# A three-layer graph network on one Trainium2 core: 16 dense chunks moved from the second and third mean pass into the first, with a new layout of PSUM banks and small tables

## The chip, the cores and the metric

The program runs on one core of a Trainium2 chip. The time is the device time of one execution in microseconds (us); a lower time is better. The engines are PE (TensorE, matmuls), DVE (VectorE), ACT (ScalarE), POOL (GpSimd, here mainly the issuer of indirect transfers) and SP (SyncE, the issuer of plain transfers). Each works through its own instruction queue in order and waits there on semaphores.

## What is computed

There are 50,000 nodes with 128 features and 25,000 edges (`src`, `dst`). Two parts follow one another, each with a residual and a row-wise layer norm:

```python
def _sage_conv(x, src, dst, Wl, bl, Wr):
    msg = x[src]
    summed = jax.ops.segment_sum(msg, dst, num_segments=N_NODES)
    cnt = jax.ops.segment_sum(jnp.ones((src.shape[0],), x.dtype), dst, num_segments=N_NODES)
    mean = summed / jnp.maximum(cnt, 1.0)[:, None]
    return mean @ Wl.T + bl + x @ Wr.T
...
x = _layernorm(x + three _sage_conv with relu between them)
x = _layernorm(x + edge attention, summed by src and projected)
```

The second part gathers queries, keys and values per edge, takes a softmax over the edges of each source node and adds the result to the node. The change lies in the first part alone.

## The kernel before

Work is cut into chunks of 512 rows (4 tiles of 128). 25,000 edges make 49 edge chunks (`NC`), 50,000 nodes make 98 node chunks (`NN`). The program has these stages: a sort of the edges by destination and by source; three **mean passes** `mean0`, `mean1`, `mean2`, one per layer; a pass `dst` over the nodes that receive edges; `attend`; and `rest`. The change touches the three mean passes and shares its helpers with `dst`.

**A mean chunk.** POOL gathers 4 tiles of source rows into `GX` (`mean_gather`, L675; `GX` has 8 slots, so POOL can be 8 chunks ahead). PE turns them (`mean_turn`: transposes at L774 in `mean0`, a matmul L890 and L892 in the later passes). DVE makes a running sum within each destination (`mean_seg`, L1396). ACT copies the turned rows into `hsrc` (`mean_keep`). PE multiplies by the left weights (`mean_prod`, L900), DVE divides by the edge count (`mean_scale`, L1403), SP stores the result. In `mean0` ACT's copy comes after the scan, in the later passes before it.

**A look-up chunk**, in `mean0` and `dst`. DVE makes one-hot rows (`look_hot_rows`, L1440), PE multiplies them with a small table (`look_up`, L929), DVE picks four columns (`look_take`, L1449) and casts them into `lookup` (L1456), which the gathers of `mean1` and `mean2` use. Before the first look-up of `mean0` a table is made on DVE and PE (`make_table`, `table_sums`); it is passed to `run` as `middle`.

**A dense chunk** treats 512 nodes that receive no edge: load of `x` (SP), transposes (`chain_t`, L774), two layers (`chain_1`, `chain_2`, L852), the last layer (`chain_y`, L870 and L872), each with an ACT copy between them; then DVE adds `x` (`add_x`, L1350), measures (L1358, L1363), ACT takes the inverse root, DVE normalises (`norm`, L1374), and SP stores. The first 49 dense chunks run in `mean1`, the other 49 in `mean2`, none in `mean0`.

**What sets the order.** `run(eng, phase, stages, count)` writes one software pipeline per engine: in step s it emits, for each stage (lead, function), the function for chunk s + lead, in the order of the list. On PE in `mean0` a step is turn(s+7), look-up(s), product(s+6); on DVE scan(s+7), scale(s+6), one-hot(s+1), take(s). In `mean1` and `mean2` the dense stages lead by 6 to 9 steps and the turn by 3, so that after the last dense `chain_y` only the turns of the last 3 chunks are left. A wait is written as a signal and how many chunks ago it must have been given: `look_up` in `mean0` waits for the take of 2 chunks ago, since it writes banks (0, 1) and (6, 7) in turn:

```python
pe.wait_ge(look_hot.of(c), look_hot.after(c))
pe.wait_ge(look_done.of(c), look_done.after(c, 2 if c.phase == "mean0" else 1))
```

The small tables and one-hot rows lie in the space of `XN`, the buffer of the dense chunks' rows, which is why SP loads no `x` before the last take of `mean0` (`look_done.end(sp, "mean0")`). Between two passes POOL waits until every product is stored (`m_stored.end`).

## Time and profile before

| | us |
|---|---|
| median of 3 runs | 2648.06 (2647.51 to 2650.15) |
| the profiled execution, its own time | 2644.61 |
| its span | 2642.8 |
| PE busy | 1873.9 (71%) |
| DVE busy | 1729.4 (65%) |
| ACT busy | 1095.2 (41%) |
| POOL busy | 1770.9 (67%) |

These are means over stages with different limits. The running sums of `mean0` start between 192.1 and 420.0 us of the span; the gathers of `mean1` begin at 429.3, those of `mean2` at 760.1, those of `dst` at 1069.5, and the last stage ends at the span's end. The granted clock of PE was 0.854 of full speed over the span. Of a row below, the first number is the start in us, the second how long the engine was busy with the group; what stands in brackets is the idle time just before it and what ended it.

### The profile page before, as it was taken

To read this page: it belongs to the slowest core of one execution; us is meant where nothing else is said; L and a number is where in the kernel's file an instruction comes from. 1 tells how busy PE (TensorE), PEld (TensorE's weight loads), DVE (VectorE), ACT (ScalarE), POOL (GpSimd) and SP (SyncE) were. 2 spreads that over 40 slices of the span, in tenths; PEclk is the share of its full clock that TensorE was granted. 3 is DMA by queue.
4 is the path that set the end of the run, shared out by engine and by line. 5 is a ranking of instruction groups with operands and counts; after the bars stand their busy time and mean duration, and the time that the engine had idled before them with its cause. 6 is when DMAs were issued, how large, how long until landed. Compare 5 with 4: busy or idle time off the path is not lost.

```text
span 2642.8 us, 43434 instructions
## 1 busy us (share of the span) xinstructions
PE 1873.9 (71%) x10441; PEld 1316.8 (50%) x10441; DVE 1729.4 (65%) x5671; ACT 1095.2 (41%) x2508; POOL 1770.9 (67%) x1895
## 2 busy tenths in 40 slices
PE   4755666999989999677777673888788877770000
PEld 2324565666656666455555453555555555540000
DVE  7787886777767777565555533888888878881000
ACT  7951111544534444122222222777666666650000
POOL 0046776566756676467777777777777777766776
PEclk7558999999999999788888885999999999995555
DMA  0025666788877887545445623455445445433321
GB/s 19 1 56 148 165 159 138 174 195 189 177 172 187 189 192 173 154 125 135 126 128 142 164 68 106 144 158 157 144 143 152 145 140 152 140 104 104 94 92 51
DMA packets 366730, 357.03 MB, mean 135 GB/s; under 512 B 46534, under 2 KB 288724, under 8 KB 366584
## 3 DMA queue, kind: packets, MB, share of 16 engines
q1 hardware_dynamic: 310136, 246.40, 31.0%
q0 software_dynamic: 56448, 109.10, 20.3%
q14 instruction: 106, 0.87, 0.1%
q8 instruction: 40, 0.66, 0.1%
HBM read 232.83 MB, written 129.11 MB: 137 GB/s over the span
## 4 chain that ended last, share of the span: by engine, by line
PE 32%; POOL 26%; issue 17%; DVE 13%; DMA 5%; ACT 5%; POOLq 1%; DVEq 0%; SPq 0%; ACTq 0%
POOL GX L675 10%; POOL hsrc L675 9%; PE bank L852 9%; PE bank L872 5%; POOL out_dram L729 4%; PE bank L774 3%; PE bank L900 3%; PE bank L892 3%; PE bank L890 3%; DMA GX<-in_x_dram,idx_a 3%; PE bank L856 2%; ACT normed L1021 2%; ACT normed L1022 2%; DVE stats L1358 2%; POOL x_prime L729 2%
## 5 line engine op out<-in xcount | busy, mean ns | idle before, releaser
L675 POOL DMA_INDIRECT GX<-mean_product,idx_a x392 | 411.2, 1049 | 129.5 <-issue 113.9
L675 POOL DMA_INDIRECT GX<-in_x_dram,idx_a x392 | 378.1, 965 | 117.9 <-issue 108.9
L852 PE MATMUL bank<-h,wt 128*128 128x512 f32 x588 | 321.0, 657 | 0.1
L1046 ACT ACTIVATE logv<-mv,eps 128x4 f32<-128x4 f32 x245 | 72.2, 295 | 541.5 <-DVE mv L1363 541.4
L729 POOL DMA_INDIRECT x_prime<-normed,idx_b x196 | 197.6, 1008 | 88.0 <-issue 83.4
L729 POOL DMA_INDIRECT out_dram<-XN,idx_b x196 | 192.8, 984 | 76.0 <-issue 64.8
L675 POOL DMA_INDIRECT hsrc<-x_prime,idx_d x196 | 189.7, 968 | 59.7 <-issue 59.7
L675 POOL DMA_INDIRECT GX<-in_edge_attr_dram,idx_a x196 | 189.7, 968 | 58.6 <-issue 53.5
L675 POOL DMA_INDIRECT hsrc<-x_prime,idx_c x196 | 186.7, 953 | 59.7 <-issue 59.7
L774 PE MATMUL bank<-ident,GX 128*128 128x128 f32 x588 | 104.5, 307 | 155.5 <-DMA GX<-in_x_dram,idx_a 149.5
L774 PE MATMUL bank<-ident,hsrc 128*128 128x128 f32 x468 | 86.5, 316 | 119.0 <-DMA hsrc<-x_prime,idx_d 57.4
L872 PE MATMUL bank<-wt,h 128*128 128x128 f32 x1176 | 170.3, 288 | 0.0
L1139 ACT ACTIVATE normed<-bank,shift,rstd 128x128 f32<-128x128 f32 x392 | 147.7, 457 | 44.9 <-DVE shift L1553 44.9
L900 PE MATMUL bank<-wt,seg 128*128 128x128 f32 x1176 | 158.5, 278 | 7.0 <-DVE seg L1396 3.6
L1374 DVE TENSOR_SCALAR normed<-res,mv,rstd 128x128 f32<-128x128 f32 x588 | 163.1, 344 | 0.0
L1345 DVE TENSOR_TENSOR res<-bank,GX 128x512 f32<-128x512 f32 x49 | 33.9, 691 | 196.9 <-PE bank L872 196.6
L856 PEld LDWEIGHTS bank<-ident,hsrc 128*128 128x128 f32 x784 | 129.0, 233 | 67.4 <-issue 67.4
L774 PEld LDWEIGHTS bank<-ident,GX 128*128 128x128 f32 x588 | 73.9, 155 | 171.6 <-issue 88.3
L774 PE MATMUL bank<-ident,XN 128*128 128x128 f32 x784 | 130.2, 293 | 41.0 <-DMA XN<-x_prime 24.2
L872 PEld LDWEIGHTS bank<-wt,h 128*128 128x128 f32 x1176 | 142.3, 191 | 33.3 <-issue 33.3
L1396 DVE TENSOR_TENSOR_SCAN seg<-flag,seg,hsrc 128x512 f32<-128x512 bf16 x98 | 126.1, 1286 | 48.0 <-ACT hsrc L1061 48.0
L900 PEld LDWEIGHTS bank<-wt,seg 128*128 128x128 f32 x1176 | 144.2, 193 | 9.0 <-DVE seg L1396 8.6
(231 smaller groups left out, 4656.0 us busy)
## 6 DMA issues: line engine op xcount, KB each, us to landing
mean_product<-prod SPq DMA_DIRECT2D x147, 256.0 KB, 4.3
hsrc<-mean_product SPq DMA_DIRECT2D x147, 256.0 KB, 4.4
XN<-in_x_dram SPq DMA_DIRECT2D x98, 256.0 KB, 4.5
x_prime<-normed SPq DMA_DIRECT2D x98, 256.0 KB
XN<-x_prime SPq DMA_DIRECT2D x98, 256.0 KB, 4.5
out_dram<-normed SPq DMA_DIRECT2D x98, 256.0 KB
flag<-same_dst_row SPq DMA_DIRECT2D x147, 128.0 KB, 4.3
XN<-low_row SPq DMA_DIRECT2D x98, 128.0 KB
```

What stands on the lines that cost most here:

```text
L675: pool.indirect_dma_start(buf[:, c.slot(U), t, :], None, table, bass.IndirectOffsetOnAxis(ap=idx[:, c.slot(U), t:t + 1], axis=0)).then_inc ...
L729: pool.indirect_dma_start(table, bass.IndirectOffsetOnAxis(ap=idx_b[:, c.slot(U), t:t + 1], axis=0), rows[:, t, :], None, bounds_check=N - ...
L774: return pe.transpose(dst, src, ident[0:src.shape[0], 0:src.shape[0]])
L852: last = pe.matmul(psum[:, :], wt[:, T_R[i], :], before[:, c.slot(2), :], start=True, stop=not dst_phase)
L856: last = pe.matmul(psum[:, t * P:(t + 1) * P], PL[:, c.slot(U), i, t, :], ident[:, :], start=False, stop=t == TPC - 1)
L872: last = pe.matmul(y[:, t * P:(t + 1) * P], h2[:, c.slot(2), t * P:(t + 1) * P], wt[:, T_R[2], :], start=False, stop=t == TPC - 1)
L890: pe.matmul(psum[:, :], wt[:, T_R[i], :], take_cols(hsrc, c.index() * CH, CH), start=True, stop=False)
L892: last = pe.matmul(psum[:, t * P:(t + 1) * P], GX[:, c.slot(U), t, 0:D], ident[:, :], start=False, stop=t == TPC - 1)
L900: last = pe.matmul(bank[3 + c.slot(2)][:, t * P:(t + 1) * P], seg[:, c.slot(2), t * P:(t + 1) * P], wt[:, T_L[int(c.phase[-1])], :], start ...
L1139: last = act.activation(normed[:, node.slot(4), t, :], norm_rows(node)[:, t, :], ACT.Identity, bias=shift[:, s, t:t + 1], scale=rstd[:, s, ...
L1374: last = dve.tensor_scalar(normed[:, c.slot(4), t, :], norm_rows(c)[:, t, :], mv[:, s, t, 0:1], rstd[:, s, t:t + 1], ALU.subtract, ALU.mult)
L1396: dve.tensor_tensor_scan(seg[:, c.slot(2), :], flag[:, c.slot(4), :], rows, seg[:, before.slot(2), CH - 1:CH], ALU.mult, ALU.add).then_inc ...
```

## The change

1. `BEFORE = 16` dense chunks run in `mean0`, (98 - 16) / 2 = 41 in each of `mean1` and `mean2` (49 before).
2. In `mean0` all mean and look-up stages lead by 5 more steps (`TABLE = 5`), so the dense chunks 0 to 15 come behind the table; `middle` is placed by a new argument `at`.
3. PSUM: the dense chunks need banks 0, 1, 2 and 6 in `mean0`. So the turn has bank 5 alone (5 and 2 before), the product bank 3 alone in `mean0` (3 and 4), the look-up banks 4 and 7 alone (two pairs before), the dense result bank 6 alone in `mean0`.
4. The waits follow: the turn waits for the copy and the scan of 1 chunk ago, the look-up for the take of 1 chunk ago (2 before), the product for the scale of 1 chunk ago in `mean0`.
5. The one-hot rows move into `res` and have one buffer instead of two, in `mean0` and in `dst`; the tables move out of `XN` into the spent raw weights. SP's wait for the last take ahead of the loads of `mean1` goes away.

```diff
@@ run
-def run(eng, phase, stages, count, to_end=True, middle=None):
+def run(eng, phase, stages, count, to_end=True, middle=None, at=0):
...
     for s in range(-max(lead for lead, _, _ in stages), 0):
+        if middle and s == -at:
+            middle()
         single(s)
-    if middle:
-        middle()
...
+    EACH = (NN - BEFORE) // 2
...
+        low_all = sb("low_all", [P, 2, CH], BF16)
+        picked = sb("picked", [P, TPC, WIDE], BF16)
+        spent = wraw[:, 0:6, :].rearrange("p a d -> p (a d)")
...
+        hot = res[:, 2, :, :].rearrange("p t d -> p (t d)").bitcast(BF16).rearrange("p (a n) -> p a n", a=2)
...
-        def turn_bank(c):
-            return (5, 2)[c.slot(2)]
+        def prod_bank(c):
+            return bank[3] if c.phase == "mean0" else bank[3 + c.slot(2)]
+        def y_bank(c):
+            return bank[6] if c.narrow else bank[6 + c.slot(2)]
...
         def first(f):
-            return lambda c: f(At("dense", c.j, c.u))
+            return lambda c: f(At("dense", c.j, c.u + BEFORE))
...
-            run(sp, "mean0", [(LAG + 3, flag_load), (2, low_load), (LAG, prod_store)], NC)
-            look_done.end(sp, "mean0")
+            run(sp, "mean0", [(TABLE + LAG + 3, flag_load), (TABLE + 2, low_load), (TABLE + LAG, prod_store),
+                              (8, zeroth(x_load), BEFORE), (0, zeroth(x_store), BEFORE)], NC)
...
             def mean_turn(c):
                 pe.wait_ge(gathered.of(c), gathered.after(c))
+                pe.wait_ge(m_h.of(c), m_h.after(c, 1))
                 if c.phase == "mean0":
-                    pe.wait_ge(m_h.of(c), m_h.after(c, 2))
-                    pe.wait_ge(m_seg.of(c), m_seg.after(c, 2))
+                    pe.wait_ge(m_seg.of(c), m_seg.after(c, 1))
+                psum = bank[5]
...
             def mean_prod(c):
                 pe.wait_ge(m_seg.of(c), m_seg.after(c))
-                pe.wait_ge(m_scaled.of(c), m_scaled.free(c))
+                pe.wait_ge(m_scaled.of(c), m_scaled.after(c, 1 if c.phase == "mean0" else 2))
...
             def look_banks(c):
-                return ((0, 1), (6, 7))[c.slot(2)] if c.phase == "mean0" else (3, 4)
+                return (4, 7) if c.phase == "mean0" else (3, 4)
             def look_up(c):
                 pe.wait_ge(look_hot.of(c), look_hot.after(c))
-                pe.wait_ge(look_done.of(c), look_done.after(c, 2 if c.phase == "mean0" else 1))
+                pe.wait_ge(look_done.of(c), look_done.after(c, 1))
...
-                    run(pe, "mean0", [(LAG + 1, mean_turn), (0, look_up), (LAG, mean_prod)], NC, middle=table_sums)
+                    run(pe, "mean0", [(TABLE + LAG + 1, mean_turn), (TABLE, look_up), (TABLE + LAG, mean_prod),
+                                       (4, zeroth(chain_t), BEFORE), (3, zeroth(chain_1), BEFORE),
+                                       (2, zeroth(chain_2), BEFORE), (1, zeroth(chain_y), BEFORE)], NC,
+                        middle=table_sums, at=TABLE + 1)
...
-                    run(act, "mean0", [(0, mean_keep)], NC)
+                    run(act, "mean0", [(TABLE + LAG + 1, mean_keep), (4, zeroth(keep_t), BEFORE), (3, zeroth(keep_1), BEFORE),
+                                        (2, zeroth(keep_2), BEFORE), (1, zeroth(inverse_root), BEFORE)], NC)
...
             def look_hot_rows(c):
                 s = c.slot(2)
                 dve.wait_ge(low_in.of(c), low_in.after(c))
-                dve.wait_ge(look_sum.of(c), look_sum.after(c, 2))
+                dve.wait_ge(look_sum.of(c), look_sum.after(c, 1))
...
-                    run(dve, "mean0", [(LAG + 1, mean_seg), (LAG, mean_scale), (1, look_hot_rows), (0, look_take)], NC,
-                        middle=make_table)
+                    run(dve, "mean0", [(TABLE + LAG + 1, mean_seg), (TABLE + LAG, mean_scale), (TABLE + 1, look_hot_rows),
+                                        (TABLE, look_take), (1, zeroth(add_x), BEFORE), (0, zeroth(norm), BEFORE)], NC,
+                        middle=make_table, at=TABLE + 1)
```

The stage lists of `mean1` and `mean2` differ only in the count `EACH` behind each dense stage.

How the order changes on PE inside `mean0`. Before, two steps of the loop (L774 turn, L929 look-up, L900 product):

```order
L774 MATMUL bank2<-ident,GX 128x128 x4
L929 MATMUL bank0<-XN 128x196 x8
L929 MATMUL bank1<-XN 128x196 x8
L897 REGISTER_ALU
L900 MATMUL bank3<-wt,seg 128x128 x4
L774 MATMUL bank5<-ident,GX 128x128 x4
L929 MATMUL bank6<-XN 128x196 x8
L929 MATMUL bank7<-XN 128x196 x8
L897 REGISTER_ALU
L900 MATMUL bank4<-wt,seg 128x128 x4
```

Of the change, one step that carries a dense chunk, and the start of the next (L777 is the transpose, L855 the two layers, L873 and L875 the last layer of the dense chunk):

```order
L777 MATMUL bank5<-ident,GX 128x128 x4
L929 MATMUL bank4<-wraw,res 128x196 x8
L929 MATMUL bank7<-wraw,res 128x196 x8
L900 MATMUL bank3<-wt,seg 128x128 x4
L777 MATMUL bank0<-ident,XN 128x128 x4
L855 MATMUL bank1<-h0,wt 128x512
L855 MATMUL bank2<-h1,wt 128x512
L873 MATMUL bank6<-b2row,ones3 128x512
L875 MATMUL bank6<-wt,h2 128x128 x4
L777 MATMUL bank5<-ident,GX 128x128 x4
L929 MATMUL bank4<-wraw,res 128x196 x8
L929 MATMUL bank7<-wraw,res 128x196 x8
```

The look-up stands ahead of the product in both. Its banks were (0, 1) and (6, 7) in turn and are 4 and 7 in every step now, and the dense matmuls stand behind the product in 16 of the steps.

On DVE, of the change, a step of `mean0` with a dense chunk (L1402 scan, L1409 scale, L1446 one-hot, L1455 take, L1462 cast, L1356 add, L1364 and L1369 measure, L1380 normalise):

```order
L1402 SCALAR_TENSOR_TENSOR seg<-flag,seg,bank5 128x512
L1409 TENSOR_TENSOR prod<-bank3,col_f 128x512
L1446 TENSOR_SCALAR res<-low_all,low_bias 128x512 x2
L1455 SCALAR_TENSOR_TENSOR picked,wraw<-count,wraw,bank4 128x196 x2
L1455 SCALAR_TENSOR_TENSOR picked,wraw<-count,wraw,bank7 128x196 x2
L1462 CAST lookup<-wraw 128x4
L1356 TENSOR_TENSOR res<-bank6,XN 128x512
L1364 BN_STATS stats<-res 128x6 x4
L1369 BN_AGGR mv<-stats 128x2 x4
L1380 TENSOR_SCALAR normed<-res,mv,rstd 128x128 x4
```

The first six rows stand in every step as before; the last four are new there and stand behind the cast.

## Rows read from the trace of the kernel before

**Rows 1.** Windows of `mean0` and `mean1`: length, busy us per engine, PE clock, DMA share, GB/s

```profile
core 0: us, PE busy (x) PEld busy (x) DVE busy (x) ACT busy (x) POOL busy (x), PEclk, DMA share, GB/s
223.00:420.00 197.00, 129.87 (x1168) 118.86 (x1169) 163.76 (x534) 24.49 (x41) 145.82 (x162) 0.95 0.63 158
466.00:753.00 287.00, 285.60 (x1621) 197.52 (x1620) 226.14 (x697) 135.84 (x272) 181.14 (x179) 1.00 0.82 183
```

**Rows 2.** Timeline of `mean0`, one step: scale, one-hot, look-up, cast, next scale

```profile
352.45 0.67 DVE L1403 TENSOR_TENSOR prod<-bank,col_f 128x512 f32<-128x512 f32 x1
353.03 0.68 DVE L1440 TENSOR_SCALAR XN<-XN,low_bias 128x512 bf16<-128x512 bf16 x2
...
354.49 1.53 PE L929 MATMUL bank<-XN 128*128 128x196 bf16 x16
...
355.31 0.17 DVE L1456 CAST lookup<-XN 128x4 f32 x1 [0.24 <-DVE XN L1449]
...
357.11 0.69 DVE L1403 TENSOR_TENSOR prod<-bank,col_f 128x512 f32<-128x512 f32 x1 [0.25 <-PE bank L900]
```

**Rows 3.** Timeline of `mean1`, one full step on PE and DVE

```profile
600.02 1.88 PE L852 MATMUL bank<-h,wt 128*128 128x512 f32 x4
...
603.15 1.06 PE L900 MATMUL bank<-wt,seg 128*128 128x128 f32 x8
...
603.35 0.69 DVE L1350 TENSOR_TENSOR res<-bank,XN 128x512 f32<-128x512 f32 x1 [0.76 <-PE bank L872]
...
605.39 1.11 DVE L1374 TENSOR_SCALAR normed<-res,mv,rstd 128x128 f32<-128x128 f32 x4
...
605.79 0.60 PE L774 MATMUL bank<-ident,XN 128*128 128x128 f32 x4
...
606.23 1.88 PE L852 MATMUL bank<-h,wt 128*128 128x512 f32 x4
```

**Rows 4.** Timeline around the table in `mean0`

```profile
209.43 0.65 DVE L1440 TENSOR_SCALAR XN<-XN,low_bias 128x512 bf16<-128x512 bf16 x2 [2.58 <-DMA XN<-low_row]
...
222.91 0.06 DVE L1433 MEMSET XN<- 128x1 f32 x1
...
231.60 1.28 DVE L1396 TENSOR_TENSOR_SCAN seg<-flag,seg,bank 128x512 f32<-128x512 bf16 x1
```

**Rows 5.** Timeline from the last gather of `mean0` to the first transposes of `mean1`

```profile
411.33 0.94 POOL L675 DMA_INDIRECT GX<-in_x_dram,idx_a  x1 [0.30 <-issue]
...
419.95 1.28 DVE L1396 TENSOR_TENSOR_SCAN seg<-flag,seg,bank 128x512 f32<-128x512 bf16 x1
...
424.93 0.69 DVE L1403 TENSOR_TENSOR prod<-bank,col_f 128x512 f32<-128x512 f32 x1 [0.88 <-PE bank L900]
...
440.69 0.17 DVE L1456 CAST lookup<-XN 128x4 int32<-128x4 f32 x1 [0.15 <-DVE XN L1449]
...
443.95 1.09 PE L774 MATMUL bank<-ident,XN 128*128 128x128 f32 x4 [4.90 <-DMA XN<-in_x_dram]
```

**Rows 6.** Timeline of the end of `mean1`: scans 39, 46 and 48, gather of chunk 43

```profile
706.14 1.32 DVE L1396 TENSOR_TENSOR_SCAN seg<-flag,seg,hsrc 128x512 f32<-128x512 bf16 x1 [0.36 <-ACT hsrc L1061]
...
706.20 0.96 POOL L675 DMA_INDIRECT GX<-mean_product,idx_a  x1 [0.60 <-POOL idx_a L665]
...
746.80 1.28 DVE L1396 TENSOR_TENSOR_SCAN seg<-flag,seg,hsrc 128x512 f32<-128x512 bf16 x1 [0.18 <-ACT hsrc L1061]
...
752.51 1.28 DVE L1396 TENSOR_TENSOR_SCAN seg<-flag,seg,hsrc 128x512 f32<-128x512 bf16 x1 [0.99 <-ACT hsrc L1061]
```

**Rows 7.** Timeline of the head of `dst`: a cast and the look-up behind it

```profile
1100.36 0.17 DVE L1456 CAST lookup<-XN 128x4 int32<-128x4 f32 x1 [0.15 <-DVE XN L1449]
...
1100.67 1.87 PE L929 MATMUL bank<-dst_table,XN 128*128 128x256 bf16 x8 [2.20 <-DVE lookup L1456]
```

**Rows 8.** PE at either clock: a look-up right after the table, and two windows

```profile
224.31 2.82 PE L929 MATMUL bank<-XN 128*128 128x196 bf16 x16
...
250.00:260.00 10.00, 5.78 (x56) 5.31 (x56) 9.30 (x31) 1.79 (x3) 7.56 (x9) 1.00 0.74 179
1080.00:1100.00 20.00, 9.33 (x40) 5.17 (x40) 10.36 (x48) 0.00 (x0) 15.43 (x18) 0.50 0.35 94
```

More of the change, by code:

```diff
@@ L38 @@
 DENSE = 5
+BEFORE = 16
+TABLE = 5
 LINE = 256
@@ L138, in run @@
     for s in range(-max(lead for lead, _, _ in stages), 0):
+        if middle and s == -at:
+            middle()
         single(s)
-    if middle:
-        middle()
-    with eng.Fori(0, whole) as j:
-        for u in range(U):
-            for lead, f, _ in stages:
-                f(At(phase, j, u + lead))
+    if whole:
+        with eng.Fori(0, whole) as j:
+            for u in range(U):
+                for lead, f, _ in stages:
+                    f(At(phase, j, u + lead))
     for s in range(whole * U, count):
@@ L867, in chain_y @@
                 pe.wait_ge(u2_kept.of(c), u2_kept.after(c))
-                pe.wait_ge(added.of(c), added.free(c))
-                y = bank[6 + c.slot(2)]
+                pe.wait_ge(added.of(c), added.after(c, 1 if c.narrow else 2))
+                y = y_bank(c)
                 pe.matmul(y[:, :], ones3[:, :], b2row[:, :, :].rearrange("k t d -> k (t d)"), start=True, stop=False)
@@ L1340, in add @@
                 s = c.slot(2)
-                y = by_tile(bank[6 + c.slot(2)][:, :])
+                y = by_tile(y_bank(c)[:, :])
                 dve.wait_ge(y_done.of(c), y_done.after(c))
@@ L1387, in mean_seg @@
                     dve.wait_ge(m_turned.of(c), m_turned.after(c))
-                    rows = bank[turn_bank(c)][:, :]
+                    rows = bank[5][:, :]
                 else:
```

69 lines of the change are left out of this document (29 added, 40 removed).

## The prediction

> **What bounds the kernel now.** I read the windows of the stages first, since the page's busy shares are means over stages with different limits. In `mean1` PE is busy 285.60 of 287.00 us at full clock, and `mean2` is the same pass again [rows 1]. So a dense chunk taken out of `mean1` or `mean2` shortens PE's queue at the bound. In `mean0` PE is busy 129.87 of 197.00 us and DVE 163.76 [rows 1]: 67 us free on PE, 33 on DVE. That is the room into which the change puts 16 dense chunks. POOL's gathers cost 0.94 + 0.31 us each, 5.0 per chunk (rows 5 show the last one of `mean0`); POOL also sets the pace of the second half of `mean0`. Second view: the timeline of one step in each pass, for the loops of waits between PE and DVE. Third: the two ends of the passes, for who is late there.
>
> The sum is made in the profiled execution (2644.61 us, span 2642.8), and 3.4 us are added at the end for the median (2648.06).
>
> **A loop closes in `mean0`.** Before, the look-up on PE runs while DVE still takes the previous one, since it has a second pair of banks. In the change it waits for that take and its cast. PE's queue then has look-up and product, and DVE's next scale waits for the product; behind the scale stand one-hot, take and cast, and the cast releases the next look-up. Each link has a row. From scale to the cast's end: 352.45 to 355.48, 3.03 us. From look-up to the next scale, released by PE's product: 354.49 to 357.11, 2.62 us [rows 2]. From a cast to the look-up that waits for it: `dst` already has this wait, 1100.53 to 1100.67, 0.14 us [rows 7]. Sum 5.8 us per step. The scan (1.28 us) hides behind look-up and product.
>
> Rule against row: the Trainium skill ("TensorE: Matmul & The Clock Gate", section "HAM oscillation — how this bites in real kernels") reports a kernel in which double-buffering PSUM "gave no further gain"; by that, taking the second banks away would cost nothing, which is the third rival below. No run here shows it yet.
>
> **A step with a dense chunk** has on DVE, behind the cast, add to normalise: 603.35 to 606.50, 3.15 us [rows 3]. DVE's queue is then 1.28 + 3.03 + 3.15 = 7.46 us. PE's is turn 0.60, look-up 1.53, product 1.06 and dense 603.15 - 600.02 = 3.13 plus its transposes 0.60, together 6.9 us [rows 2, 3]. DVE is the longer, and PE's dense matmuls cover the wait of the loop. So 7.46. The first dense step has no normalise: 1.28 + 3.03 + 2.04 = 6.35. The last has only a normalise (1.11 us), which fits into the 5.8. The single turn bank costs nothing while the copy (behind the scan) ends some 3 us ahead of the next look-up; if it did not, PE would start the look-up late and every step would pay.
>
> **Sum for `mean0`, from scan 8 on.** Before, scan 8 starts at 231.60 [rows 4] and scan 48 at 419.95 [rows 5], 188.35 us for 40 steps.
> - Table. The step behind the table has one scan and scale fewer ahead of it and the one-hot behind it. DVE is free at 209.43 - 2.58 = 206.85 [rows 4]; less that scan, scale and their wait, 2.3, the table begins at 204.55 in place of 210.0, 5.4 earlier, but about 3.2 of scan, scale, one-hot and waits come behind it. Scan 8: 2.2 us earlier.
> - 40 steps: 24 x 5.8 + 6.35 + 15 x 7.46 = 257.4, in place of 188.35: +69.1.
> - Scan 48 to scale 48: before 4.98 (419.95 to 424.93); now one loop to the cast (5.8) and 0.14 + 2.62: 8.5, +3.5. POOL's gathers of `mean1` wait for this product.
> - The six last look-ups: before, the last cast ends at 440.86, 15.9 behind scale 48 [rows 5]. Now scale to cast 3.03 and six times look-up 1.53, two latencies of 0.1, one-hot, take and cast 2.45 (353.03 to 355.48), 4.2 us, less 0.6 as the last has no one-hot: 27.6, +11.7.
> - The rows `x` for `mean1` are loaded ahead now. Before, PE's first transposes start 3.1 us behind the last cast and end a wait for that DMA [rows 5]; now about 0.2: -2.9. SP has five stages per step in its queue: the store of a dense chunk waits for the normalise, and the low-row load of the next step stands behind it; it is needed a full step (over 5 us) later, so nothing.
>
> Together the first dense work of `mean1` starts 79.2 us later. POOL starts its gathers 70.4 later and has its 8 slots full before PE asks, so it is covered.
>
> **Sum for `mean1` and `mean2`.** A full step is 6.21 us (600.02 to 606.23) [rows 3]. Eight fewer put the last step with dense work at 746.80 - 49.7 = 697.1, in the times of before. From there 10 more turns at (752.51 - 746.80) / 2 = 2.86 us [rows 6] would end at 725.7. But POOL is late next: the gather of chunk 43 starts when turn 39 frees its slot (706.20 beside scan 39 at 706.14 [rows 6]), then 5 more at 5.02, and from the start of a last gather to its scan 8.6 us (411.33 to 419.95 [rows 5]), some 1.1 more here, as turn and copy come ahead of the scan. 697.1 + 2.9 + 25.1 + 9.7 = 734.8 in place of 752.51: 17.7 us per pass, 35.4 for both. Unhidden ends for this: 26.8 per pass (POOL not late), and 12 if the gathers keep the 6 us that many have under load. I take 17.7, since rows 5 are a drained tail like this one.
>
> **`dst`.** The one-hot has one buffer and now stands in the loop of look-up and cast: 0.34 us [rows 2] for the 7 look-ups ahead of the first dense work: +2.4.
>
> **Total:** 79.2 - 35.4 + 2.4 = +46.2 us. 2644.6 + 46.2 = 2690.8; with the 3.4 of the median 2694.
>
> **Bounds.** A mean-only step of `mean0` is between DVE's busy time, 163.76 / 41 = 4.0 us [rows 1], and 8.1, the loop at half clock (below). I take 5.8, the sum of its links. A dense step is between 6.9 (PE) and 8.5 (a wait of 1 us at each end of the add).
>
> **Rivals.**
> - *PE's clock falls (slower).* In the loop PE is busy 3.2 of 5.8 us. At 5.78 of 10 us it still had the full clock of 2.4 GHz, at 9.33 of 20 it had 0.50, 1.2 GHz [rows 8], and after an idle stretch a look-up took 2.82 us in place of 1.53. If it stays down, 24 steps cost 1.29 + 1.06 more each, +56 us: 2750; half of that if it swings. The last six look-ups are the likeliest place: 1.3 each, 8 us. The Trainium skill (same page, section "A second HAM failure mode: psum-queue depth-cycling") says short pauses between groups of matmuls make the clock swing; the row with 5.78 speaks against it here.
> - *POOL is not late at the ends of `mean1` and `mean2`.* 26.8 per pass in place of 17.7: 2676. Against it stands the free-running pitch of 5.0 us, beside 2.86.
> - *The loop stays open (faster).* If the second buffers were idle slack, DVE's queue alone would set `mean0`: 24 x 4.0 and 16 x 7.15 make 210.4, +22; nothing for the six look-ups. -2.2 + 22.0 - 2.9 - 35.4 + 2.4 = -16.1: 2632. With the measured 4.3 us of an unblocked step it would be 2643, no difference. The point of decision is a mean-only step of 4.3 us: above it the change is slower. For it speaks that the dense work does go to a stage with 67 us of free PE time; against it, that `dst` shows this very wait, 2.20 us idle ahead of each look-up [rows 7].
>
> **Chances.** Forecast 0.68 (its own range 2680 to 2712), clock 0.14, POOL not late 0.10, loop open 0.08. The range 2664 to 2730 takes in the second rival and half of the first; it leaves out the open loop, the full clock loss and a few errors of size. A measurement of this kernel can tell 0.2%, 5 us, from no change. Faster 0.06 and same 0.03 are the open loop at its two prices, with a little for an error in the sum; slower 0.91.
>
> **What the profile of the changed kernel would show.** Casts of `mean0` 5.8 us apart without and 7.5 with a dense chunk; PE idle before each look-up, released by the cast (DVE), not the one-hot; scale released by PE's product. The gathers of `mean1` start near 500 us, first transposes at 523. In `mean1` and `mean2` 32 full steps of 6.2, then turns at 2.9, then at 5 waiting for the gather DMA; first gathers of `mean2` near 820, of `dst` near 1113. `attend` unchanged. The prediction is wrong if scans of `mean0` come 4.3 us apart in mean-only steps, if they come 7 to 8 apart with the clock near 0.5, or if the last turns of `mean1` never wait for POOL.

## The result and the profile after

The changed kernel takes 2736.48 us (median of 6 runs, 2732.89 to 2739.44) where the kernel before, on the same chip, takes 2648.57 (6 runs, 2646.49 to 2652.07): ratio 1.033, 95% interval 1.0317 to 1.0343. It is slower, as forecast, but by 88 us where the forecast had 46, and outside its range. The profiled execution takes 2734.38 us with a span of 2732.1; the span of before is 2642.8, so 89.3 us are to be placed.

The page of the changed kernel first: busy times, the PE clock in 40 slices, and three groups of its fifth part (busy and mean ns of one, then the idle time before them and what ended it).

```profile
PE 1908.8 (70%) x10441; PEld 1345.7 (49%) x10441; DVE 1732.4 (63%) x5671; ACT 1092.1 (40%) x2508; POOL 1774.0 (65%) x1895
...
PEclk7568987799998999878888887799999999995555
...
L678 POOL DMA_INDIRECT GX<-mean_product,idx_a x392 | 409.2, 1044 | 126.6 <-issue 110.9
L678 POOL DMA_INDIRECT GX<-in_x_dram,idx_a x392 | 379.5, 968 | 122.8 <-issue 109.1
...
L929 PE MATMUL bank<-wraw,res 128*128 128x196 bf16 x784 | 106.4, 309 | 92.2 <-DVE lookup L1462 91.9
```

DVE is as busy as before (1732.4 against 1729.4): nothing was added to its work. PE has 35 us more (1908.8 against 1873.9) for the same matmuls, and sits idle for 92.2 us ahead of the look-ups of `mean0`. A busy time that grows without new work is a sign of a lower clock, and the windows show where. Columns as in [rows 1].

```profile
core 0: us, PE busy (x) PEld busy (x) DVE busy (x) ACT busy (x) POOL busy (x), PEclk, DMA share, GB/s
240.00:360.00 120.00, 106.87 (x756) 79.95 (x755) 109.90 (x416) 44.41 (x94) 65.28 (x72) 1.00 0.59 168
360.00:507.00 147.00, 89.12 (x590) 80.85 (x588) 89.64 (x299) 13.04 (x23) 69.24 (x77) 0.77 0.46 114
571.00:848.00 277.00, 263.13 (x1483) 184.31 (x1482) 202.63 (x593) 117.34 (x233) 181.41 (x179) 0.98 0.82 174
506.00:549.00 43.00, 21.33 (x144) 18.07 (x144) 19.95 (x94) 0.60 (x1) 20.75 (x24) 0.71 0.52 121
```

The first is `mean0` with dense chunks, the second `mean0` without, the third `mean1`, the last the six look-ups at the end of `mean0`. With dense chunks beside it PE keeps 1.00. Without, and among the last look-ups, it gets 0.77 and 0.71, between its two levels of 1.2 and 2.4 GHz (0.50 and 1.00), where before the whole of `mean0` had 0.95 [rows 1].

| span from, to | before | after | difference | forecast |
|---|---|---|---|---|
| start to scan 8 | 231.6 | 229.7 | -1.9 | -2.2 |
| 40 steps, scan 8 to scan 48 | 188.4 | 277.5 | +89.1 | +69.1 |
| scan 48 to the last cast | 20.7 | 42.2 | +21.5 | +15.2 |
| last cast to scan 0 of `mean1` | 25.0 | 22.0 | -3.0 | -2.9 |
| `mean1`, scan 0 to scan 48 | 286.8 | 277.2 | -9.7 | -17.7 |
| `mean2`, the same | 286.8 | 277.3 | -9.5 | -17.7 |
| between the passes, `dst` and the rest | | | +2.8 | +2.4 |
| sum | 2642.8 | 2732.1 | +89.3 | +46.2 |

The form of the forecast holds in every line. 26.5 of the 43 us that it lacks are in `mean0`, 16.2 at the ends of `mean1` and `mean2`.

**A step without a dense chunk.** Timeline of the changed kernel; [rows 2] show one of before.

```profile
458.86 0.37 DVE L1462 CAST lookup<-wraw 128x4 int32<-128x4 f32 x1
459.06 1.28 DVE L1402 TENSOR_TENSOR_SCAN seg<-flag,seg,bank 128x512 f32<-128x512 bf16 x1
...
459.38 2.77 PE L929 MATMUL bank<-wraw,res 128*128 128x196 bf16 x16 [2.85 <-DVE lookup L1462]
...
461.94 1.24 PE L900 MATMUL bank<-wt,seg 128*128 128x128 f32 x8
...
463.22 0.69 DVE L1409 TENSOR_TENSOR prod<-bank,col_f 128x512 f32<-128x512 f32 x1 [2.88 <-PE bank L900]
463.82 0.61 DVE L1446 TENSOR_SCALAR res<-low_all,low_bias 128x512 bf16<-128x512 bf16 x2
```

This is the loop of the forecast, link by link: PE waits 2.85 us for the cast, DVE waits 2.88 us for the product, one at a time. But the look-up takes 2.77 us where the forecast had 1.53, much as the first look-up behind the table did before (2.82 us, [rows 8]). Most such steps are 6.8 to 7.1 us apart, 6.78 on average.

This is not a clock that is down in one step and up in the next. Of the look-ups 21 to 41 of `mean0`, 16 of 21 take 2.77 us and one takes 1.52 (mean 2.64); the products behind them take 1.39 us on average where 1.06 to 1.08 is the time at full clock and 1.92 to 1.96 at half. So in nearly every step the look-up, right behind the wait, runs at half clock, and the product mostly at full clock again.

**The same loop stood in the trace of before.** At the head of `dst` each look-up waits for a cast, 2.20 us, and takes 1.87 us [rows 7]; the clock granted from 1100 to 1108 us is 0.50. A few steps on, with dense work on PE and no wait, the same eight matmuls need little more than half. Timeline of before:

```profile
1109.37 1.04 PE L929 MATMUL bank<-dst_table,XN 128*128 128x256 bf16 x8
```

So the kernel before already had the price of a look-up behind such a wait.

**A step with one.** Same view, 150 us earlier:

```profile
312.05 0.17 DVE L1462 CAST lookup<-wraw 128x4 int32<-128x4 f32 x1
312.15 0.69 DVE L1356 TENSOR_TENSOR res<-bank,XN 128x512 f32<-128x512 f32 x1
312.37 1.52 PE L929 MATMUL bank<-wraw,res 128*128 128x196 bf16 x16 [0.94 <-DVE lookup L1462]
...
319.07 0.17 DVE L1462 CAST lookup<-wraw 128x4 int32<-128x4 f32 x1
```

The look-up waits only 0.94 us and takes 1.52. DVE waits nowhere; the step takes 7.02 us, a little under the 7.46 of the forecast.

**The end of `mean0`.** The last look-ups, with nothing else left on PE ([rows 5] have the last cast of before):

```profile
540.45 0.29 DVE L1462 CAST lookup<-wraw 128x4 int32<-128x4 f32 x1 [0.15 <-DVE picked L1455]
540.89 2.77 PE L929 MATMUL bank<-wraw,res 128*128 128x196 bf16 x16 [2.67 <-DVE lookup L1462]
545.88 0.17 DVE L1462 CAST lookup<-wraw 128x4 int32<-128x4 f32 x1
546.20 1.53 PE L929 MATMUL bank<-wraw,res 128*128 128x196 bf16 x16 [2.54 <-DVE lookup L1462]
549.37 0.17 DVE L1462 CAST lookup<-wraw 128x4 int32<-128x4 f32 x1 [0.15 <-DVE picked L1455]
```

One look-up ran at half clock and needed 5.4 us from cast to cast, the next at full clock and needed 3.5, here with no one-hot behind it. Three of the last six look-ups take 2.77 us.

**The end of `mean1`.** Timeline of POOL's index copies (L668) and gathers (L678), with turns (PE L890) and scans (DVE L1402); [rows 6] have the same place before.

```profile
786.38 0.21 POOL L668 COPY idx_a<-lookup 128x16 int32 x1 [2.15 <-PE bank L892]
787.24 1.69 POOL L678 DMA_INDIRECT GX<-mean_product,idx_a  x1 [0.65 <-POOL idx_a L668]
...
808.95 0.83 POOL L668 COPY idx_a<-lookup 128x16 int32<-128x16 int32 x1
809.94 0.96 POOL L678 DMA_INDIRECT GX<-mean_product,idx_a  x1 [0.16 <-POOL idx_a L668]
...
815.76 2.08 PE L890 MATMUL bank<-hsrc,wt 128*128 128x512 f32 x2 [4.11 <-DMA GX<-mean_product,idx_a]
...
820.30 1.28 DVE L1402 TENSOR_TENSOR_SCAN seg<-flag,seg,hsrc 128x512 f32<-128x512 bf16 x1 [7.07 <-ACT hsrc L1066]
...
835.26 0.95 POOL L678 DMA_INDIRECT GX<-mean_product,idx_a  x1 [0.30 <-issue]
...
848.52 1.28 DVE L1402 TENSOR_TENSOR_SCAN seg<-flag,seg,hsrc 128x512 f32<-128x512 bf16 x1 [3.26 <-ACT hsrc L1066]
```

The copy at 786.38 holds gather 39 until turn 35. From there POOL never waits again: the copy at 808.95 and gather 43 at 809.94 follow without a wait for PE, 238.6 us behind scan 0 (571.4). Scan 39, which the forecast took as what frees gather 43, was at 234.3. POOL is 4.3 us late there by its own queue. And from the start of gather 48 (835.26) to scan 48 pass 13.3 us.

**What makes a gather slow on POOL.** The mean of a gather issue is 1044 ns from `mean_product` and 968 ns from `x`, and single ones take up to 1.94 us. In `mean1` and `mean2` of the changed kernel all 43 issues of over 1.2 us (of 392) began while DVE ran a scan. Issues that begin 0.1 to 1.0 us into a scan end 0.75 to 0.77 us behind that scan's end, all 54 of them. The last issue of gather 48 is one:

```profile
838.90 1.28 DVE L1402 TENSOR_TENSOR_SCAN seg<-flag,seg,hsrc 128x512 f32<-128x512 bf16 x1 [3.06 <-ACT hsrc L1066]
...
839.01 1.93 POOL L678 DMA_INDIRECT GX<-mean_product,idx_a  x1 [0.30 <-issue]
```

In `mean0`, where the scan reads a PSUM bank in place of `hsrc`, 24 issues began in the same part of a scan and none took over 0.97 us. All 14 kernels of this text show the same (54 to 66 issues each, ends 0.75 to 0.79 us behind the scan, none in `mean0`). No run changed the scan's source alone, so that this is what matters is argued from the two kinds of pass. In sum it costs POOL some 20 us per late pass: the issues take that much longer than 0.94 us each.

### The profile page after: what moved, and what is told of

Same layout as the page of the kernel before. It is cut to its first block, busy times and chain, and to the rows that moved or that the text cites. A ratio compares the mean times of both kernels' runs of the same rounds, so it can differ in the third digit from the quotient of the medians.

```text
span 2732.1 us, 42310 instructions
## 1 busy us (share of the span) xinstructions
PE 1908.8 (70%) x10441; PEld 1345.7 (49%) x10441; DVE 1732.4 (63%) x5671; ACT 1092.1 (40%) x2508; POOL 1774.0 (65%) x1895
## 4 chain that ended last, share of the span: by engine, by line
PE 33%; POOL 25%; issue 16%; DVE 15%; DMA 5%; ACT 5%; POOLq 1%; DVEq 0%; SPq 0%; ACTq 0%
POOL hsrc L678 11%; POOL GX L678 8%; PE bank L855 8%; PE bank L875 4%; POOL out_dram L732 4%; PE bank L900 4%; PE bank L929 4%; PE bank L777 3%; DVE picked L1455 3%; PE bank L892 3%; PE bank L890 2%; DMA GX<-in_x_dram,idx_a 2%; PE bank L859 2%; ACT normed L1026 2%; ACT normed L1027 2%
## 5 line engine op out<-in xcount | busy, mean ns | idle before, releaser
L678 POOL DMA_INDIRECT GX<-mean_product,idx_a x392 | 409.2, 1044 | 126.6 <-issue 110.9
L678 POOL DMA_INDIRECT GX<-in_x_dram,idx_a x392 | 379.5, 968 | 122.8 <-issue 109.1
L855 PE MATMUL bank<-h,wt 128*128 128x512 f32 x588 | 319.0, 653 | 0.4 <-ACT h L1040 0.3
L678 POOL DMA_INDIRECT hsrc<-x_prime,idx_d x196 | 191.7, 978 | 59.8 <-issue 59.8
L678 POOL DMA_INDIRECT hsrc<-x_prime,idx_c x196 | 187.2, 955 | 59.8 <-issue 59.8
L678 POOL DMA_INDIRECT GX<-in_edge_attr_dram,idx_a x196 | 187.1, 955 | 58.6 <-issue 53.8
L777 PE MATMUL bank<-ident,GX 128*128 128x128 f32 x588 | 102.0, 301 | 133.4 <-DMA GX<-in_x_dram,idx_a 116.8
L1402 DVE TENSOR_TENSOR_SCAN seg<-flag,seg,hsrc 128x512 f32<-128x512 bf16 x98 | 126.0, 1286 | 89.2 <-ACT hsrc L1066 89.0
L929 PE MATMUL bank<-wraw,res 128*128 128x196 bf16 x784 | 106.4, 309 | 92.2 <-DVE lookup L1462 91.9
L900 PE MATMUL bank<-wt,seg 128*128 128x128 f32 x1176 | 168.0, 289 | 3.8 <-DVE prod L1409 3.8
L875 PE MATMUL bank<-wt,h 128*128 128x128 f32 x1176 | 170.3, 288 | 0.0
L777 PE MATMUL bank<-ident,hsrc 128*128 128x128 f32 x468 | 86.1, 315 | 117.3 <-DMA hsrc<-x_prime,idx_d 53.3
L1380 DVE TENSOR_SCALAR normed<-res,mv,rstd 128x128 f32<-128x128 f32 x588 | 163.8, 349 | 0.0
L875 PEld LDWEIGHTS bank<-wt,h 128*128 128x128 f32 x1176 | 142.3, 191 | 33.3 <-issue 33.3
L900 PEld LDWEIGHTS bank<-wt,seg 128*128 128x128 f32 x1176 | 155.8, 206 | 4.8 <-DVE seg L1402 4.1
L777 PE MATMUL bank<-ident,XN 128*128 128x128 f32 x784 | 128.9, 290 | 38.2 <-DMA XN<-x_prime 24.3
```

The lines of the kernel that those rows point to most:

```text
L678: pool.indirect_dma_start(buf[:, c.slot(U), t, :], None, table, bass.IndirectOffsetOnAxis(ap=idx[:, c.slot(U), t:t + 1], axis=0)).then_inc ...
L777: return pe.transpose(dst, src, ident[0:src.shape[0], 0:src.shape[0]])
L855: last = pe.matmul(psum[:, :], wt[:, T_R[i], :], before[:, c.slot(2), :], start=True, stop=not dst_phase)
L875: last = pe.matmul(y[:, t * P:(t + 1) * P], h2[:, c.slot(2), t * P:(t + 1) * P], wt[:, T_R[2], :], start=False, stop=t == TPC - 1)
L900: last = pe.matmul(prod_bank(c)[:, t * P:(t + 1) * P], seg[:, c.slot(2), t * P:(t + 1) * P], wt[:, T_L[int(c.phase[-1])], :], start=True, ...
L929: last = pe.matmul(to, rows[:, t * P:(t + 1) * P], table, start=k == 0, stop=k == len(pairs) - 1)
```

## The experiments

All are edits of the changed kernel if nothing else is said; ratios are to the kernel before, run on the same chip beside them. Its time differs a little from one such set to the next (2644.03 us beside e1 to e4, 2646.80 beside e5 to e8, 2647.24 beside e9 to e12), so what an edit gives back is counted over it: the change costs 87.9 us. "Scan 48 to last cast" ends at that cast's start. The stretches of their profiled executions, in us:

| | 40 steps | scan 48 to last cast | `mean1` | `mean2` | span |
|---|---|---|---|---|---|
| before | 188.4 | 20.7 | 286.8 | 286.8 | 2642.8 |
| changed | 277.5 | 42.2 | 277.2 | 277.3 | 2732.1 |
| e1 product first | 218.9 | 38.4 | 279.3 | 278.5 | 2678.0 |
| e2 two pairs | 224.6 | 23.6 | 279.9 | 279.1 | 2668.8 |
| e3 layout alone | 271.5 | 43.0 | 286.8 | 286.8 | 2749.5 |
| e4 busy PE | 249.6 | 35.1 | 278.2 | 278.3 | 2697.1 |
| e5 both, 16 chunks | 220.7 | 20.6 | 278.6 | 278.6 | 2654.9 |
| e6 both, 6 chunks | 199.9 | 20.4 | 280.4 | 281.5 | 2636.1 |
| e7 other rows | 274.6 | 42.6 | 277.2 | 277.5 | 2732.3 |
| e8 both, 10 chunks | 207.0 | 22.5 | 281.1 | 278.8 | 2649.6 |
| e9 changed, gather first | 277.4 | 42.2 | 276.0 | 275.7 | 2731.3 |
| e10 as e6, gather first | 201.1 | 23.0 | 276.8 | 276.7 | 2632.5 |
| e11 as e8, gather first | 207.9 | 22.0 | 277.9 | 276.8 | 2640.7 |
| e12 before, gather first | 191.1 | 21.0 | 286.8 | 286.8 | 2645.4 |

### Experiment 1: PE's product ahead of the look-up

```diff
-run(pe, "mean0", [(TABLE + LAG + 1, mean_turn), (TABLE, look_up), (TABLE + LAG, mean_prod),
+run(pe, "mean0", [(TABLE + LAG + 1, mean_turn), (TABLE + LAG, mean_prod), (TABLE, look_up),
...
```

> The changed kernel, with PE's product ahead of the look-up in every step of mean0 (it was behind it); waits and banks are left as they are. Loop theory: the scale no longer waits for a product that stands behind the look-up, so the loop of cast, look-up, one-hot, take and cast is 4.2 us beside DVE's own 4.3; the 24 mean-only steps of mean0, 6.9 us apart in the changed kernel, come to 4.3 to 5.0, some 45 to 58 us less in all, a median of 2680 to 2690. Rival, dense load: DVE's added work in mean0 is what costs; then the order on PE changes nothing beyond 5 us, 2730 to 2740. Dense steps stay at 7.1 us under both.

Measured: 2673.05 us (4 runs), ratio 1.011 (1.0093 to 1.0127). That is 29.0 us over the kernel before: one exchange in a list gives back 59 of the 88 us, a little more than expected. The window and one step of it:

```profile
400.00:420.00 20.00, 14.28 (x134) 12.64 (x135) 18.88 (x58) 2.98 (x5) 15.27 (x18) 1.00 0.71 166
```

```profile
408.58 0.17 DVE L1462 CAST lookup<-wraw 128x4 int32<-128x4 f32 x1
408.89 1.52 PE L929 MATMUL bank<-wraw,res 128*128 128x196 bf16 x16 [0.98 <-DVE lookup L1462]
409.13 1.28 DVE L1402 TENSOR_TENSOR_SCAN seg<-flag,seg,bank 128x512 f32<-128x512 bf16 x1 [0.38 <-issue]
410.33 0.67 DVE L1409 TENSOR_TENSOR prod<-bank,col_f 128x512 f32<-128x512 f32 x1
...
463.09 2.77 PE L929 MATMUL bank<-wraw,res 128*128 128x196 bf16 x16 [2.53 <-DVE lookup L1462]
```

The look-up still waits for the cast, with its single pair of banks. But the scale no longer stands behind it, so DVE is hardly idle (busy 18.88 of 20 us), most steps are 4.1 to 4.4 us apart, and the clock is 1.00. It takes both to close the loop: the single pair, and the product that stands behind the look-up in PE's queue. The last look-ups, where no product is left to exchange, stay nearly as slow as they were (38.4 us in place of 42.2, the look-up of 463.09 at 2.77).

### Experiment 2: a second pair of banks once the dense chunks are through

`paired(c, n)` is true in `mean0` from chunk n on; the take reads the banks by the same rule.

```diff
-return (4, 7) if c.phase == "mean0" else (3, 4)
...
+return (0, 1) if paired(c, 20) and c.slot(2) else (4, 7)
...
-pe.wait_ge(look_done.of(c), look_done.after(c, 1))
+pe.wait_ge(look_done.of(c), look_done.after(c, 2 if paired(c, 21) else 1))
```

> The changed kernel, with a second pair of look-up banks (0 and 1, free once the 16 dense chunks are through) from look-up 20 of mean0 on; the one-hot keeps its one buffer and PE its order. Loop theory: the look-up again runs beside the take, mean-only steps come to 4.3 to 5.0 us (22 of them, 42 to 57 us less) and the six last look-ups go from 23 us to some 14; median 2670 to 2685. Rival, one-hot: if the single one-hot buffer is what binds, nothing changes, 2730 to 2740. Rival, dense load: no change either.

Measured: 2666.32 us (4 runs), ratio 1.0082 (1.0065 to 1.0098), 22.3 us over the kernel before. In one step:

```profile
408.45 1.52 PE L935 MATMUL bank<-wraw,res 128*128 128x196 bf16 x16
...
409.82 1.08 PE L904 MATMUL bank<-wt,seg 128*128 128x128 f32 x8
409.87 0.17 DVE L1468 CAST lookup<-wraw 128x4 int32<-128x4 f32 x1 [0.15 <-DVE picked L1461]
410.07 1.28 DVE L1408 TENSOR_TENSOR_SCAN seg<-flag,seg,bank 128x512 f32<-128x512 bf16 x1
```

The look-up starts without a wait, while DVE still takes the one before it (its cast is the one at 409.87); most steps are 4.1 to 4.4 us from look-up 21 on, and the end takes 23.6 us, near the 20.7 of before. So the second pair is worth 66 us here. The two repairs reach the same steps by different ways: e1 and e2 both open the loop, and either is enough in the steps; only the second pair brings the last six look-ups back (18.7 us; e1 gives 3.9). The Trainium skill ("TensorE: Matmul & The Clock Gate", section "HAM oscillation — how this bites in real kernels") reports one kernel in which double-buffering PSUM "gave no further gain", as weighed in the prediction. That does not carry over to this kernel, where the second pair gives 66 us.

### Experiment 3: the new layout without dense chunks in `mean0`

```diff
-BEFORE = 16
+BEFORE = 0
```

In addition the dense stages are left out of the lists of `mean0`; 49 dense chunks run in `mean1` and 49 in `mean2`, as before.

> The new layout, leads and waits with no dense chunk in mean0 (49 in each later pass, as before the change). Loop theory: all 40 steps of mean0 behind scan 8 take the 6.9 us of the mean-only steps, 276 us in place of 188, the six last look-ups 10 us more, dst 3 more, and nothing is saved in mean1 and mean2: 2745 to 2760, slower than the changed kernel. Rival, dense load: without dense work mean0 is back at some 190 us and the whole is within 10 us of the kernel before, 2645 to 2660.

Measured: 2747.88 us (4 runs), ratio 1.0393 (1.0376 to 1.0411), slower than the change itself. The layout and its waits cost 106.7 us of span alone; the 16 dense chunks give back 17.4. In `mean0` they cost 6.0 us in the 40 steps (277.5 against 271.5), since the loop leaves both engines idle anyway, and the later passes are 9.6 and 9.5 shorter.

### Experiment 4: PE kept busy in the wait

Three matmuls of 256 columns into a bank that nobody reads, behind each product of the steps from look-up 20 on.

```diff
+for k in range(3):
+    pe.matmul(bank[0][:, 0:256], ident[:, :], wt[:, 0:2, :].rearrange("p a d -> p (a d)"), start=True, stop=True)
```

> The changed kernel, with three matmuls of 256 columns that nobody reads (into bank 0) at the end of each PE step of mean0 from look-up 20 on, to keep PE busy in its wait for the cast. Clock theory: the look-up of a mean-only step takes 2.8 us because the granted clock falls in each wait; with PE busy it is 1.5, the step 5.8 in place of 6.9, 22 steps and the six last look-ups some 25 to 32 us less: 2705 to 2715, with a clock of 1.00 in place of 0.76 in the windows from 380 to 500 us. Rival, pure waits: the clock is not what lengthens the step; the added matmuls lie in the wait and the time stays at 2736, or rises by up to 40 if they do not fit.

Measured: 2700.22 us (4 runs), ratio 1.0217 (1.02 to 1.0234), 56.2 us over the kernel before: added work made the kernel 32 us faster. Window and look-up:

```profile
380.00:400.00 20.00, 16.01 (x132) 14.50 (x130) 14.22 (x44) 2.39 (x4) 11.79 (x14) 1.00 0.54 131
```

```profile
407.23 1.52 PE L929 MATMUL bank<-wraw,res 128*128 128x196 bf16 x16 [1.39 <-DVE lookup L1467]
```

At a clock of 1.00 the same closed loop takes 5.5 to 5.7 us per step, where the forecast had 5.8, and the look-up 1.52, from look-up 22 on in every step. This separates the two costs. The loop costs 5.6 - 4.3 = 1.3 us per step, and the clock that falls in its waits about 1.2 more. The granted clock was 0.76 in the window of 380 to 400 us of the changed kernel.

### Experiments 5, 6 and 8: both repairs, with 16, 6 and 10 dense chunks in `mean0`

The edits of e1 and e2 (the second pair from look-up 20, 10 or 14 on, behind the dense chunks), two buffers for the one-hot of `dst`, and `BEFORE` of 16, 6 or 10. Of the `dst` part, the wait:

```diff
-dve.wait_ge(look_sum.of(c), look_sum.after(c, 1))
+dve.wait_ge(look_sum.of(c), look_sum.after(c, 1 if c.phase == "mean0" else 2))
```

> The changed kernel with both repairs: product ahead of the look-up, the second pair of look-up banks from look-up 20 on, and in dst two one-hot buffers (the unused half of the one). If the loop was the whole loss, this beats the kernel before (2644 in the last call) by the 19 us saved in mean1 and mean2. If a dense chunk in mean0 also costs what DVE needs for it (7.1 us per step beside some 4.7 before, 16 times 2.4 = 38), it stays slower: 2648 to 2660.

> As the kernel with both repairs, but 6 dense chunks in mean0 and 46 in each later pass. DVE's spare time in mean0 before (33 of 197 us, of which POOL's pace of 5.0 us beside DVE's 4.3 leaves some 20) holds about 6 chunks of 3.1 us, so mean0 stays within 10 us of before, and 3 steps of 6.2 less per later pass save 2 times 8 to 10: 2628 to 2640, faster than before by 0.2 to 0.6%. If the gathers are late as soon as any dense chunk is taken out, or mean0 grows by 2.4 us per chunk from the first on, it is 2640 to 2655.

> As the kernel with both repairs, with 10 dense chunks in mean0 and 44 in each later pass. mean0 grows by DVE's excess, about 10 to 15 us, the later passes save 2 times 9 to 10: 2635 to 2648, between the kernels with 6 and with 16.

Measured: 16 chunks 2652.9 us (10 runs), ratio 1.0027 (1.0017 to 1.0036); 10 chunks 2646.65 (10 runs), 0.9993 (0.9984 to 1.0003); 6 chunks 2637.91 (5 runs), 0.9966 (0.9952 to 0.998). With both repairs the idea of the change is nearly neutral at 16 (0.27% slower) and pays a little at 6 (0.34% faster). The reason is in the table. A dense chunk in `mean0` lengthens its step from 4.1 to 7.1 us. Ten more (6 to 16) cost 20.8 us there, less than 10 x 3.0, since with 6 the 40 steps go at POOL's pace (199.9 us, 5.0 each) and turns wait for gathers. In return, 5 fewer full steps in each pass bring only 1.8 and 3.0 us, not 3.3 x 5: the passes end on POOL by then.

### Experiment 7: gathers of `mean1` and `mean2` from other rows

```diff
-stage(c, idx_ready, (idx_a, col_i[:, V_SRC_A, :] if c.phase == "mean0" else lookup[:, :]))
+stage(c, idx_ready, (idx_a, col_i[:, V_SRC_A, :]))
```

In addition the gather always reads `x`, so these passes sum other rows than they should.

> The changed kernel, whose gathers of mean1 and mean2 read rows of x by the source index of mean0 and not rows of the product tables (so these passes compute on other rows): same count and size of transfers, other addresses. Theory, slow addresses: a gathered packet takes 0.32 us in mean1 and 0.13 in mean0 because most look-ups point at the few zero rows behind the product table; with spread rows it takes under 0.2 in mean1, the last gathers land 2 to 3 us behind their issue in place of 7, and each late pass ends 6 to 8 us earlier (277 to some 270): 2718 to 2726. Rival, dense traffic: loads and stores of the dense chunks slow the gathers; then packets stay at 0.3 us and the time at 2732 to 2740.

Measured: 2732.66 us (4 runs), ratio 1.0322 (1.0304 to 1.0341), as the changed kernel. The gathers' queue in `mean1`, 571 to 848 us (packets, MB, share of 16 engines), of the changed kernel and then of this one:

```profile
q0 software_dynamic: 5376, 11.02, 39.3%
```

```profile
q0 software_dynamic: 5376, 11.02, 15.9%
```

The same number of packets and bytes takes 39.3% of 16 engines for 277 us, 0.32 us a packet, in the one and 15.9%, 0.13 us, in the other. So the rows that `mean1` really reads are 2.5 times as slow to fetch. Yet the pass takes 277.2 us in both, where 6 to 8 us less were expected. This does not clear the slow packets. Chunk 42, the first that the turns wait for, is scanned 244.0 us behind scan 0 in place of 248.9, and from the end of the last issue to scan 48 pass 5.5 us in place of 7.6. But the scans now come at other times, five issues of gathers 44 to 48 are held by one (1.24 to 1.87 us each) where one was for so long (1.93 us), and the last issue ends at 271.7 in place of 269.6. Quicker packets gave 2.05 us at the end, and slower issues took 2.15.

### Experiments 9 to 12: POOL's gather ahead of its index copy

The copy of four chunks' indices waits for the turn 8 chunks before the last of the four, and stood in POOL's queue ahead of a gather that needed none of this: the copy for chunks 44 to 47 waits for turn 39 and holds gather 43, whose own slot turn 35 had freed.

```diff
-run(pool, f"mean{i}", [(1, block_of(mean_stage)), (0, mean_gather)], NC)
+run(pool, f"mean{i}", [(0, mean_gather), (1, block_of(mean_stage))], NC)
```

> The changed kernel with one exchange in POOL's order of the mean passes: the gather of a chunk is emitted ahead of the copy of the next four chunks' indices, in place of behind it. That copy waits for the turn of the chunk 8 ahead of the block's last, so in the changed kernel gathers 35, 39, 43 stand behind the waits for turns 31, 35, 39; in mean1 gather 39 starts 215.9 us behind scan 0, released by turn 35, gather 43 at 238.6, with POOL never idle between, and scan 48 comes at 277.2. Theory A (the tail is set by how late POOL is when the dense work ends): gather 39 no longer stands behind turn 35, gathers 40 to 48 come 5 us earlier, scan 48 of mean1 and of mean2 near 272.3; together 9 to 11 us: 2726 against 2736.5. Theory B (the landing of the gathers under load decides, and POOL's start does not): last turns as late as before, 277 in both passes, 2736. Mean0's 40 steps unchanged (277) under both.

> The version with 6 dense chunks in mean0, product first, two bank pairs and two dst one-hots (2637.9 us), with the same exchange on POOL. Theory A: its passes take 280.4 and 281.5 from scan 0 to scan 48 with POOL late from about turn 43 on; 5 us earlier each, but not under the end that PE's queue sets, 43 dense steps at 6.2 and turns at 2.9, so 3 to 5 us per pass: 2629 to 2632. Theory B: 2638.

> The version with 10 dense chunks in mean0 (2646.7 us, passes of 281.1 and 278.8), with the same exchange. Theory A: 5 us per pass, 2636 to 2638. Theory B: 2647.

> The kernel before with the same exchange. There the dense work lasts to about scan 46 at 281.1, and the last two turns follow at 2.9 us without a wait for POOL: gather 43 starts at 240.5 behind turn 39, gather 48 at 270.3. Theory A: gathers 5 us earlier, nothing at the end of mean1 or mean2 (286.8 stays), at most 1 or 2 us at the end of mean0, where POOL sets the pace of the second half: 2643 to 2648. Theory B: 2648.

Measured: e9 2730.75 us (5 runs), ratio 1.0312 (1.0296 to 1.0327); e10 2634.32 (5 runs), 0.9954 (0.9941 to 0.9967); e11 2641.51 (12 runs), 0.998 (0.997 to 0.999); e12 2650.29 (12 runs), 1.0017 (1.0008 to 1.0025). All four lie 2 to 5 us above what theory A expected.

In e9 gather 39 starts 207.0 us behind scan 0, not 215.9, as theory A said, and gather 43 at 232.5, not 238.6. But gather 48 starts at 263.3 and not at 258: the lead of 6 us is used up between 43 and 48.

```profile
808.95 0.84 POOL L668 COPY idx_a<-lookup 128x16 int32<-128x16 int32 x1
810.62 0.96 POOL L678 DMA_INDIRECT GX<-mean_product,idx_a  x1 [0.83 <-PE bank L892]
813.25 0.94 POOL L678 DMA_INDIRECT GX<-mean_product,idx_a  x1 [1.67 <-issue]
814.50 1.77 POOL L678 DMA_INDIRECT GX<-mean_product,idx_a  x1 [0.30 <-issue]
```

Here POOL pauses for 1.67 us with no releaser that the profile shows, and a gather takes 1.77 us in place of 0.94. Gathers 43 to 48 are 6.2 us apart in place of 5.1. So the pass gains 1.1 and 1.6 us of the 5 expected: theory A named what is late, and its size is wrong; theory B, no gain, is wrong by a little. The trace tells where the lead went. From gather 43 to gather 48 pass 30.8 us, where five undisturbed gathers take 25.0. Some 3.7 of the 5.8 us lie in four long issues (1.30, 1.77, 1.56 and 1.45 us) that all begin in a scan, and in the pause, which begins 0.2 us into one. The other 2.1 us are the two index copies that the exchange put inside this stretch.

In e10 the exchange does what was expected. The last scans of `mean1` in e6, then in e10:

```profile
740.98 1.28 DVE L1408 TENSOR_TENSOR_SCAN seg<-flag,seg,hsrc 128x512 f32<-128x512 bf16 x1 [0.99 <-ACT hsrc L1072]
745.08 1.28 DVE L1408 TENSOR_TENSOR_SCAN seg<-flag,seg,hsrc 128x512 f32<-128x512 bf16 x1 [2.23 <-ACT hsrc L1072]
750.35 1.28 DVE L1408 TENSOR_TENSOR_SCAN seg<-flag,seg,hsrc 128x512 f32<-128x512 bf16 x1 [3.40 <-ACT hsrc L1072]
```

```profile
745.65 1.28 DVE L1408 TENSOR_TENSOR_SCAN seg<-flag,seg,hsrc 128x512 f32<-128x512 bf16 x1 [0.99 <-ACT hsrc L1072]
748.51 1.28 DVE L1408 TENSOR_TENSOR_SCAN seg<-flag,seg,hsrc 128x512 f32<-128x512 bf16 x1 [0.99 <-ACT hsrc L1072]
751.37 1.28 DVE L1408 TENSOR_TENSOR_SCAN seg<-flag,seg,hsrc 128x512 f32<-128x512 bf16 x1 [0.99 <-ACT hsrc L1072]
```

Scans at 2.86 us to the last: POOL is not late, and both passes end on PE, 3.6 and 4.8 us sooner. e10 has the lowest median of all, 2634.3 us, 0.46% under the kernel before; its interval overlaps that of e6, so the gain over e6 is seen in the passes and not in the times (`mean0` came out 3.8 us longer). In e11 the passes gain 3.2 and 2.0 us over e8. For the kernel before (e12) the exchange brings nothing at the ends of `mean1` and `mean2`, where PE is the bound to the last turn, and the run came out 0.17% slower; its profile has `mean0` 2.7 us longer.

## Why the prediction was wrong, point by point

- **What bounds each stage**: right for `mean1`, whose dense steps stay at 6.2 us. That `mean0` has room for 16 dense chunks is so only beside the closed loop, where they cost 6 us (e3). With the loop open they cost 32 us (e5, 220.7 against 188.4): 16 x 3.15 = 50 us of DVE's time do not fit into its 33 free us. The rival of an open loop, at 2632 or 2643, had 217.6 us for this with its 4.3 us step, and 17.7 per pass for the tail, where 8.2 came; e5 is at 2652.9.
- **A loop closes in `mean0`**: right in every link, and shown by two repairs that open it (e1, e2).
- **24 mean-only steps x 5.8 us**: this step failed, by size. They take 6.78 us on average (162.6 us), +23.4. The 5.8 was priced at full clock and holds at full clock (5.6 in e4). But in a closed loop PE waits some 2.6 to 2.9 us per step, the granted clock is 0.77, and the look-up behind the wait runs at half clock in nearly every step. The prediction had this as a rival, with two prices: 56 us if the clock stays down for look-up and product, and half of that if it swings. The look-up pays in full (2.64 us on average in place of 1.53) and the product little (1.39 in place of 1.06), so 23.4 and the clock's part of the last look-ups, 6.3, come to about that half. The row that spoke against it, 5.78 of 10 us busy at clock 1.00 [rows 8], is from a stage with PE's work in short pieces; here PE is busy 89.12 of 147 us, no smaller a share, with one long wait per step. A busy share did not tell the clock. The row that did tell it was named for the wait alone: the loop of `dst` [rows 7], from which the prediction took 0.14 us of latency and not that its look-up, behind a wait of 2.20 us, took 1.87 us where 1.04 is its time at full clock. The Trainium skill ("TensorE: Matmul & The Clock Gate", section "A second HAM failure mode: psum-queue depth-cycling") says, as cited there, that short pauses between groups of matmuls make the clock swing between its two levels. This trace agrees: a pause of 2.85 us, a look-up of 2.77, a product of 1.24.
- **16 dense steps, 6.35 + 15 x 7.46**: 114.9 us measured, -3.4; DVE is the longer queue, as said.
- **The six last look-ups, and scan 48 to its scale (+15.2)**: +21.5. Casts are 5.4, 4.6, 5.4, 4.4, 5.4 and 3.5 us apart where 4.2 was priced (less for the last), with look-ups of 2.77 us in three of the six and between 1.53 and 2.08 in the others. Same cause: e4, at full clock, has 35.1 us for the stretch in place of 42.2.
- **17.7 us per pass at the ends of `mean1` and `mean2`**: this step failed too, 9.7 and 9.5. Its words were "the gather of chunk 43 starts when turn 39 frees its slot". The reason is wrong: with 8 slots turn 35 frees that slot, and what waits for turn 39 is the index copy ahead of the gather, as [rows 6] have it (0.60 <-POOL idx_a L665). In e9, without the copy ahead of it, gather 43 starts at 232.5, before scan 39 at 234.3. The time is right for the kernel before, where the turns come every 6.2 us and POOL is through with gathers 39 to 42 when turn 39 comes. In the change scans 38 and 39 follow at 5.1 and 2.9 us, and POOL, held by the index copy until turn 35, needs 22.7 us for gathers 39 to 42: +4.3. The last gather then takes 13.3 us to its scan and not the 9.7 taken from `mean0` [rows 5]: +3.6. With 0.2 for the pitch that is the 8.1 us missing in `mean1`. Of the 3.6 us, 1.0 is one issue of 1.93 us that met a scan, and 2.6 lie between the last issue and the scan, 7.6 us where the prediction's numbers give 5.0; with quicker packets it is 5.5 (e7). Most of it has one root in the prediction: it priced POOL's issues and landings in `mean1` by rows of `mean0`, where no scan holds an issue and packets are quick. What taking away POOL's late start gives depends on what comes next: 1.1 and 1.6 us in the changed kernel (e9), 3.6 and 4.8 with 6 dense chunks (e10).
- **Table, x preloaded, `dst`**: right. The first two are within 0.3 us. The first casts of `dst` are 4.4 us apart in place of 4.1, as priced; the last line of the table (+2.8) also holds the rest of the program.
- **Chances**: the direction was never in doubt, with 0.91. The range ended at 2730 because the clock rival counted as a case of its own, of 0.14; its two prices lay at 2722 and 2750, and the tail's least gain (12 us per pass, still above the 9.7 and 9.5 that came) was not combined with either. Both happened together: 2694 + 30 + 16 = 2740, less 3.4 for the dense steps.
